# Attention and experts on one core: the weighted values of groups three and four joined, and the values' product moved behind the first two distances

## The chip, the core and the metric

The kernel runs on one core of one Trainium2 chip, in one launch. The metric is the time of that launch on the device in microseconds (us). Engines are named as the profile names them: PE is TensorE (PEld its weight loads), DVE is VectorE, ACT is ScalarE, POOL is GpSimd, SP is SyncE, which here only issues DMAs.

## The reference

One transformer layer over 32 batches of 256 tokens with 128 features. The attention has 16 heads of 8 features and replaces softmax by a rational function of the shifted logits; the expert part has four experts, of which each token uses two.

```python
x = x + attn(layernorm(x))            # qkv = x @ w_qkv.T, 16 heads of 8
    attn = einsum('bhsd,bhtd->bhst', q, k) * hd ** -0.5
    d = attn - max(attn)              # d <= 0
    s = 1 / (1 - d * (1 - 0.5 * d * (1 - d / 3)))
    out = (s / sum(s)) @ v            # then @ w_out.T + b_out
x = x + ffn(layernorm(x))
    gates = top 2 of softmax(x @ router_w + router_b), normalized
    h = silu(x @ w1[e]) * (x @ w3[e]) # 128 -> 512, for e in 0..3
    out = sum_e gates[e] * (h @ w2[e])
```

## The kernel before

Each engine has its own instruction stream, written out by hand; they meet only through semaphores (`wait_ge`, `then_inc`). Nothing reorders the work, so the order of the calls in the code is the order on the engine.

A stage number n stands for one step of a pipeline over batches. In `first_half` of step n, TensorE works on three batches: the distances of batch n (the maximum minus each score, from the scores recomputed with the row maximum as one more term), the end of the attention of batch n - 1, and the expert products of batch n - 2. In `second_half` it makes the scores of batch n + 1 for their maxima, the down products of batch n - 2, the router of batch n - 1, and the first weighted values of batch n. Steps -2 to 3 and 28 to 31 are written out, steps 4 to 27 run as a loop of 12 passes with two steps each. From step 2 on the order is the same ("settled", `settled(n)`).

The names that matter here:

- `distances(i, off, u)` (matmuls on L1380), u = 0..7: two products of 512 columns into `sc`. For u > 1 it waits for `poly_ok`, the polynomial of unit u - 2, which read the same buffer. ScalarE squares the distance (`square`, L657), VectorE makes the polynomial from square and distance (`polynomial`, L906).
- `weighted_values(i, off, g)` (L1312), g = 0..3: the weights of group g times the values, eight products in 32-column form (each recorded twice, so x16), into `pv`. It waits for `p_ok`, which ScalarE raises after the `Exp` of group g (`weights_of`, L771). ScalarE copies `pv` away after the fourth group (`values_T_copied`, L694).
- `values()` (L1405): the values of batch n + 1 into `misc`, x4 records. ScalarE copies them (`values_copied`, L688) between the second square and `silu(1)`.
- `up_a_unit`, `up_b_unit` (both L1294): six products of 256 columns each, the two factors of the hidden layer for unit u. `up_a` is read by `silu` (L666), `up_b` by `hidden` (L898). `up_a_unit(u)` waits for `silu(u - 1)`, `up_b_unit(u)` for a hidden product before it.

At the seam of two steps TensorE runs, before the change: `up_a_unit(0)`, queries and keys, `weighted_values(2)`, `up_b_unit(0)`, then in the next step `values()`, `distance(0)`, `distance(1)`, `weighted_values(3)`, `ups(1)` (both units 1), `distance(2)`, `up_a_unit(2)`, `distance(3)`, `up_b_unit(2)`, `up_a_unit(3)`, `distance(4)`. ScalarE's order in the same stretch is `silu(0)`, `square(0)`, `square(1)`, the copy of the values, `silu(1)`, the copy of `pv`, `square(2)`, `silu(2)`, `square(3)`. VectorE's is `hidden(0)`, `polynomial(0)`, `polynomial(1)`, `hidden(1)`, `polynomial(2)`, `hidden(2)`, `polynomial(3)`.

Of the kernel before, what the change touches and what calls it, by code (L numbers as in the profile page):

```python
# [5 lines left out]
def attention_then_experts_kernel(nc: bass.Bass, x: bass.AP, w_qkv: bass.AP, w_out: bass.AP, b_out: bass.AP,  # L6
# [26 lines left out]
    B, S, D = x.shape  # L33
# [25 lines left out]
    with ctx:  # L59
# [193 lines left out]
        def no(i, off):  # L253
            return 2 * i + off

        def has(i, off):
            return not isinstance(i, int) or 0 <= no(i, off) < B

        def after(eng, s, count):

            if not isinstance(count, int) or count > 0:
                eng.wait_ge(s, count)

        def settled(n):

            return not isinstance(n, int) or n >= 2
# [1010 lines left out]
        def _(pe):  # L1277
# [19 lines left out]
            def weighted_values(i, off, g):  # L1297

                n, par = no(i, off), off % 2
                pe.wait_ge(p_ok, G * n + g + 1)  # L1300
                if g == 0:
                    pe.wait_ge(v_ok, n + 1)
                    after(pe, o_ok, n)
                    if has(i, off - 2):
                        pe.wait_ge(hid_ok, UP * (n - 1))
                    if has(i, off + 1):
                        pe.wait_ge(s_used, U * (n + 1) + 6)
                first = 16 - 16 * (g % 2)
                for c in range(C):
                    for j in range(4):  # L1310
                        at = (2 * c + j % 2) * S
                        last = nc.tensor.matmul(pv[32 * j:32 * j + 32, g // 2, :],  # L1312
                                                v_pad[par][:, c, 4 * g + j, first:first + 32],
                                                poly[:, 2 * g + j // 2, at:at + S], start=(g % 2 == 0 and c == 0),
                                                stop=(g % 2 == 1 and c == C - 1))
                last.then_inc(pv_full, 1)
# [9 lines left out]
            def up_a_unit(i, off, u):  # L1326
                m = no(i, off)
                after(pe, silu_ok, UP * m + u)
                if u == 0:
                    pe.wait_ge(xn2_lo_ok, m + 1)  # L1330
                up(u, up_a, w1_hi, w1_lo, a_full)

            def up_b_unit(i, off, u):
                m = no(i, off)
                if u < 3:
                    after(pe, hid_ok, UP * m + u)
                elif u == 3:
                    pe.wait_ge(o_ok, min(m + 2, B) if isinstance(i, int) else m + 2)
                else:
                    pe.wait_ge(hid_ok, UP * m + u - 1)  # L1340
                if u == 0:
                    after(pe, acc_ok, m)
                    pe.wait_ge(lg_ok, m + 1)
                up(u, b_bank[u], w3_hi, w3_lo, b_full)
# [39 lines left out]
            def first_half(i, off):  # L1384
                n = no(i, off)

                def ups(u):
                    if has(i, off - 2):
                        up_a_unit(i, off - 2, u)
                        up_b_unit(i, off - 2, u)  # L1390

                def distance(u):
                    if has(i, off):
                        distances(i, off, u)

                def values():
                    if not has(i, off + 1):
                        return
                    m = n + 1
                    if isinstance(i, int) and m == 0:  # L1400
                        pe.wait_ge(qk_ok, 1)
                    else:
                        pe.wait_ge(qk_out, m)
                    for c in range(C):
                        last = nc.tensor.matmul(misc[:, c * D:(c + 1) * D], xn_T[:, c * 128:(c + 1) * 128],  # L1405
                                                proj_T[:, 2, :], start=True, stop=True)
                    last.then_inc(v_full, 1)
# [5 lines left out]
                def values_T():  # L1413
                    if not has(i, off - 1):
                        return
                    m = n - 1
                    pe.wait_ge(o_ok, m + 1)
                    if has(i, off + 1):
                        pe.wait_ge(v_ok, n + 2)
                    else:  # L1420
                        pe.wait_ge(xn2_out, m)
                        if has(i, off):
                            pe.wait_ge(m_ok, n + 1)
                    for c in range(C):
                        for a in range(G // 2):
                            at = (c * G // 2 + a) * 128
                            last = nc.tensor.transpose(misc[:, at:at + 128], o_T[:, a, c * 128:(c + 1) * 128], ident[:])  # L1427
                    last.then_inc(oq_full, 1)

                def attention_T():  # L1430
                    if not has(i, off - 1):
                        return
                    m = n - 1
                    pe.wait_ge(attn_ok, m + 1)
                    for c in range(C):
                        last = nc.tensor.transpose(misc[:, c * 128:(c + 1) * 128], attn[:, c, :], ident[:])
                    last.then_inc(attnT_full, 1)

                def output_projection():
                    if not has(i, off - 1):  # L1440
                        return
                    m = n - 1
                    pe.wait_ge(attnT_ok, m + 1)
                    for c in range(C):
                        last = nc.tensor.matmul(misc[:, c * D:(c + 1) * D], attn_T[:, c * 128:(c + 1) * 128],  # L1445
                                                proj_T[:, 3, :], start=True, stop=True)
                    last.then_inc(res_full, 1)

                if settled(n):
                    values()  # L1450
                    distance(0)
                    distance(1)
                    weighted_values(i, off - 1, 3)
                    ups(1)
                    distance(2)
                    up_a_unit(i, off - 2, 2)
                    distance(3)
                    up_b_unit(i, off - 2, 2)
                    up_a_unit(i, off - 2, 3)
                    distance(4)  # L1460
                    values_T()
                    up_a_unit(i, off - 2, 4)
                    distance(5)
                    up_b_unit(i, off - 2, 3)
                    up_b_unit(i, off - 2, 4)
                    up_a_unit(i, off - 2, 5)
                    distance(6)
                    attention_T()
                    up_a_unit(i, off - 2, 6)
                    distance(7)  # L1470
                    up_b_unit(i, off - 2, 5)
                    up_a_unit(i, off - 2, 7)
                    up_b_unit(i, off - 2, 6)
                    up_b_unit(i, off - 2, 7)
                    output_projection()
                    return
# [51 lines left out]
            def second_half(i, off):  # L1528
                n = no(i, off)
# [108 lines left out]
                if settled(n):  # L1638
                    score(0)
                    down(0, 0)  # L1640
                    down(0, 1)
                    score(1)
                    down(0, 2)
                    down(0, 3)
                    down(1, 0)
                    score(2)
                    down(1, 1)
                    down(1, 2)
                    router_operand()
                    score(3)  # L1650
                    down(1, 3)
                    if has(i, off + 2):
                        queries_operand()
                    weighted_values(i, off, 0)
                    weighted_values(i, off, 1)
                    if has(i, off + 1):
                        maxima_T()
                    router_logits()
                    up_a_unit(i, off - 1, 0)
                    if has(i, off + 2):  # L1660
                        queries_and_keys()
                    if isinstance(i, int) and n == B - 1:
                        up_b_unit(i, off - 1, 0)
                        late_up_a(LATE, 1)
                        late_up_b(LATE, 1)
                    weighted_values(i, off, 2)
                    if not (isinstance(i, int) and n == B - 1):
                        up_b_unit(i, off - 1, 0)
                    return

# [154 lines left out]
```

## Time and profile before

| what | value |
|---|---|
| median of 3 runs | 1122.63 us (1122.23 to 1123.55) |
| the profiled execution's own time | 1123.23 us |
| its span | 1121.5 us |
| granted TensorE clock, mean | 0.998 |
| PE busy | 1099.9 us (98%) |
| ACT busy | 995.3 us (89%) |
| DVE busy | 962.8 us (86%) |
| POOL busy | 744.1 us (66%) |
| one step in the middle of the kernel | 33.2 us |

The busy rows say how much of the span each engine had an instruction in flight. Matmuls overlap in the pipeline, so a PE that reads 98% busy can still be waiting a little between two of them; what tells is the distance from the start of one matmul to the start of the next. The last row is the distance between the same instruction in two neighbouring steps: the third group's weighted values start at 549.55 us in one step, and the row of the first two groups at 545.37 us has its like one step later at 578.53 us.

### The profile page before, as it was taken

How to read it: one execution, taken by the hardware profiler on the slowest of the kernel's cores; microseconds unless marked ns; L12 is line 12 of the kernel's file. 1: busy time of each engine (PE TensorE's matmuls, PEld its weight loads, DVE VectorE, ACT ScalarE, POOL GpSimd, SP SyncE). 2: the span in 40 equal slices, each digit the busy share in tenths (PEclk: the TensorE clock that was granted, in tenths of full speed). 3: DMA queues.
4: the chain of work that ended last, by engine and by line, in shares of the span. 5: the costliest groups of instructions: out<-in, count | busy, mean ns of one | idle time of the engine just before them, and what ended most of it. 6: DMA issues, size and time to landing. Idle time of an engine off the chain costs nothing.

```text
span 1121.5 us, 29146 instructions
## 1 busy us (share of the span) xinstructions
PE 1099.9 (98%) x9968; PEld 934.8 (83%) x9968; DVE 962.8 (86%) x1665; ACT 995.3 (89%) x1034; POOL 744.1 (66%) x936
## 2 busy tenths in 40 slices
PE   6989999999999999999999999999999999999998
PEld 5768888888888888888888888888888888888888
DVE  5789888899888899888899988889988889998844
ACT  1789999999999999999999999999999999999982
POOL 4547766777676687776677767668767667776530
PEclk9999999999999999999999999999999999999999
DMA  6343433333433223343223343322433322344000
GB/s 192 110 143 120 129 105 96 95 103 122 123 115 101 90 87 122 123 128 105 90 88 110 118 127 114 98 91 90 122 123 123 107 88 88 113 122 125 30 7 10
DMA packets 130383, 117.49 MB, mean 105 GB/s; under 512 B 15748, under 2 KB 124964, under 8 KB 130340
## 3 DMA queue, kind: packets, MB, share of 16 engines
q1 hardware_dynamic: 128004, 113.78, 32.9%
q10 hardware_dynamic: 2336, 3.15, 0.9%
q8 instruction: 26, 0.43, 0.2%
q14 instruction: 17, 0.14, 0.0%
HBM read 94.18 MB, written 21.09 MB: 103 GB/s over the span
## 4 chain that ended last, share of the span: by engine, by line
PE 93%; DVE 3%; ACT 1%; ACTq 1%; DMA 1%; issue 0%; POOL 0%; SPq 0%; POOLq 0%; DVEq 0%
PE banks L1294 33%; PE banks L1569 20%; PE sc L1380 11%; PE banks L1312 11%; PE sc L1552 4%; PE misc L1294 2%; PE banks L1603 2%; DVE mx L991 1%; PE misc L1427 1%; PE misc L1445 1%; PE misc L1405 1%; PE banks L1552 1%; PE sc L1294 1%; PE banks L1288 1%; DVE poly L906 1%; PE sc L1745 1%
## 5 line engine op out<-in xcount | busy, mean ns | idle before, releaser
L481 POOL TENSOR_TENSOR hid<-hid,gate_all 128x512 f32<-128x512 f32 x240 | 380.7, 1630 | 167.6 <-DMA gate_all<-gate_scratch 156.8
L906 DVE SCALAR_TENSOR_TENSOR poly<-w_sq,sc 128x1024 f32<-128x1024 f32 x252 | 303.5, 1215 | 46.3 <-ACT w_sq L657 46.1
L1294 PE MATMUL banks<-xn_hi,w_hi 128*128 128x256 f32 x976 | 289.5, 297 | 0.3
L1294 PE MATMUL banks<-xn_lo,w_hi 128*128 128x256 f32 x976 | 275.2, 282 | 0.0
L1294 PE MATMUL banks<-xn_hi,w_lo 128*128 128x256 f32 x976 | 274.1, 281 | 0.0
L657 ACT ACTIVATE w_sq<-sc 128x1024 f32<-128x1024 f32 x252 | 255.6, 1027 | 13.0 <-PE sc L1380 7.0
L1569 PE MATMUL banks<-w_sb,hid 128*128 128x128 f32 x1920 | 245.9, 281 | 0.4 <-POOL hid L481 0.4
L766 ACT ACTIVATE poly<-poly 128x2048 f32<-128x2048 f32 x128 | 240.2, 1899 | 0.3
L1569 PEld LDWEIGHTS banks<-w_sb,hid 128*128 128x128 f32 x1920 | 223.3, 191 | 16.5 <-POOL hid L481 0.6
L771 ACT ACTIVATE poly<-poly 128x2048 f32<-128x2048 f32 x128 | 236.8, 1896 | 0.0
L991 DVE TENSOR_REDUCE mx<-sc 128x4 f32<-128x1024 f32 x192 | 229.4, 1211 | 6.5 <-PE sc L1552 5.7
L1294 PEld LDWEIGHTS banks<-xn_hi,w_hi 128*128 128x128 f32 x976 | 183.3, 188 | 37.2 <-issue 24.3
L666 ACT ACTIVATE silu_a<-banks 128x512 f32<-128x512 f32 x240 | 144.1, 600 | 60.9 <-PE banks L1294 44.5
L1294 PEld LDWEIGHTS banks<-xn_lo,w_hi 128*128 128x128 f32 x976 | 183.8, 188 | 5.1
L1294 PEld LDWEIGHTS banks<-xn_hi,w_lo 128*128 128x128 f32 x976 | 184.2, 189 | 0.0
L898 DVE TENSOR_TENSOR hid<-silu_a,banks 128x512 f32<-128x512 f32 x240 | 161.0, 681 | 16.5 <-ACT silu_a L666 16.0
L1380 PE MATMUL sc<-q_pad,k_stack 128*128 128x512 f32 x504 | 161.2, 411 | 1.5 <-DMA q_pad<-m_split 0.8
L1312 PE MATMUL banks<-poly,v_pad 128*32 128x256 f32 x2048 | 130.6, 384 | 0.9 <-DVE mx L991 0.7
L1312 PEld LDWEIGHTS banks<-poly,v_pad 128*32 128x32 f32 x2048 | 56.7, 109 | 50.6 <-issue 17.9
L1380 PEld LDWEIGHTS sc<-q_pad,k_stack 128*128 128x128 f32 x504 | 78.8, 189 | 9.2 <-issue 1.9
L991 DVE TENSOR_REDUCE mx<-banks 128x4 f32<-128x1024 f32 x64 | 77.6, 1212 | 0.0
L1552 PE MATMUL sc<-k_tile,q_tile 32*128 32x256 f32 x768 | 64.6, 328 | 4.2 <-DVE mx L991 3.7
(186 smaller groups left out, 1338.2 us busy)
## 6 DMA issues: line engine op xcount, KB each, us to landing
qk_scratch<-qk_split SPq DMA_DIRECT2D x32, 512.0 KB, 3.1
q_pad<-qk_scratch SPq DMA_DIRECT2D x256, 64.0 KB
k_tile<-qk_scratch SPq DMA_DIRECT2D x124, 128.0 KB, 2.5
q_tile<-qk_scratch SPq DMA_DIRECT2D x124, 128.0 KB, 2.5
k_stack<-qk_scratch SPq DMA_DIRECT2D x124, 128.0 KB
gate_all<-gate_scratch SPq DMA_DIRECT2D x30, 512.0 KB, 4.4
x_in<-in_L_attn_x_dram SPq DMA_DIRECT2D x32, 128.0 KB, 2.1
x_res<-in_L_attn_x_dram SPq DMA_DIRECT2D x32, 128.0 KB, 2.2
```

The costliest lines, as they stand in the source:

```text
L481: nc.gpsimd.tensor_tensor(h, h, by_token.unsqueeze(1).to_broadcast([128, 2, C, 128]), ALU.mult).then_inc(gated, 1)
L657: nc.scalar.activation(w_sq[:, u % 2, :], distance_buf(n, u), ACT.Square).then_inc(sq_ok, 1)
L666: nc.scalar.activation(silu_a[:, u % 2, :], up_a[:], ACT.Silu).then_inc(silu_ok, 1)
L766: nc.scalar.activation(poly[:, C * g:C * (g + 1), :], poly[:, C * g:C * (g + 1), :], ACT.Ln, bias=2.0).then_inc(ln_ok, 1)
L771: nc.scalar.activation(poly[:, C * g:C * (g + 1), :], poly[:, C * g:C * (g + 1), :], ACT.Exp, scale=-1.0).then_inc(p_ok, 1)
L898: nc.vector.tensor_tensor(hid[:, 2 * u:2 * u + 2, :].rearrange("p a t -> p (a t)"), silu_a[:, u % 2, :], b_bank[u], ALU.mult).then_inc(hid ...
L906: nc.vector.scalar_tensor_tensor(poly[:, u, :], w_sq[:, u % 2, :], 3.0, distance_buf(n, u), ALU.add, ALU.mult).then_inc(poly_ok, 1)
L991: nc.vector.tensor_reduce(by_row[:, :, :, u], score_buf[u].rearrange("p (j c t) -> p j c t", j=2, c=C), AX.X, ALU.min, negate=True).then_i ...
L1294: last = nc.tensor.matmul(dst, lhs[a], rhs[b], start=(k == 0), stop=(k == len(terms) - 1))
L1312: last = nc.tensor.matmul(pv[32 * j:32 * j + 32, g // 2, :], v_pad[par][:, c, 4 * g + j, first:first + 32], poly[:, 2 * g + j // 2, at:at ...
L1380: last = nc.tensor.matmul(dst[:, 2 * c * S:2 * (c + 1) * S], k_stack[par][:, u, c * 128:(c + 1) * 128], q_pad[par][:, u, :, :].rearrange(" ...
L1569: last = nc.tensor.matmul(up_b[:, c * D:(c + 1) * D], hid[:, FB * e + f, c * 128:(c + 1) * 128], w2_sb[:, FB * e + f, :], start=(e == 0 an ...
```

## The change

In settled steps the third group's weighted values leave the second half, where they stood between queries and keys and `up_b_unit(0)`. They now open the next step's first half, directly followed by the fourth group's. Then come the first two distances, and behind those the values' product. In step 2 only the fourth group moves, since step 1 has already done the third group at the end of its own second half. In the last step (31) the third group stays in the second half. No product is added or dropped, and no wait is added: each call brings its own waits along.

```diff
                 if settled(n):
-                    values()
+                    if not (isinstance(i, int) and n == 2):
+                        weighted_values(i, off - 1, 2)
+                    weighted_values(i, off - 1, 3)
                     distance(0)
                     distance(1)
-                    weighted_values(i, off - 1, 3)
+                    values()
                     ups(1)
                     distance(2)
...
                         up_b_unit(i, off - 1, 0)
                         late_up_a(LATE, 1)
                         late_up_b(LATE, 1)
-                    weighted_values(i, off, 2)
-                    if not (isinstance(i, int) and n == B - 1):
+                        weighted_values(i, off, 2)
+                    else:
                         up_b_unit(i, off - 1, 0)
                     return
```

On TensorE, at the seam of two settled steps, this stands before (the first row is the last product of queries and keys; x8 of L1312 is one group, x4 of L1380 are distances 0 and 1):

```order
L1294 MATMUL misc<-xn_split,proj_lo 128x256
L1312 MATMUL banks<-poly,v_pad 32x256 x8
L1294 MATMUL banks<-xn_hi,w_hi 128x256
L1294 MATMUL banks<-xn_lo,w_hi 128x256
L1294 MATMUL banks<-xn_hi,w_lo 128x256
L1294 MATMUL banks<-xn_hi,w_hi 128x256
L1294 MATMUL banks<-xn_lo,w_hi 128x256
L1294 MATMUL banks<-xn_hi,w_lo 128x256
L1405 MATMUL misc<-proj_T,xn_T 128x128 x2
L1380 MATMUL sc<-q_pad,k_stack 128x512 x4
L1312 MATMUL banks<-poly,v_pad 32x256 x8
L1294 MATMUL banks<-xn_hi,w_hi 128x256
```

And this stands there now, again on TensorE and from the same product on:

```order
L1294 MATMUL misc<-xn_split,proj_lo 128x256
L1294 MATMUL banks<-xn_hi,w_hi 128x256
L1294 MATMUL banks<-xn_lo,w_hi 128x256
L1294 MATMUL banks<-xn_hi,w_lo 128x256
L1294 MATMUL banks<-xn_hi,w_hi 128x256
L1294 MATMUL banks<-xn_lo,w_hi 128x256
L1294 MATMUL banks<-xn_hi,w_lo 128x256
L1312 MATMUL banks<-poly,v_pad 32x256 x16
L1380 MATMUL sc<-q_pad,k_stack 128x512 x4
L1405 MATMUL misc<-proj_T,xn_T 128x128 x2
L1294 MATMUL banks<-xn_hi,w_hi 128x256
```

The two groups of eight have become one of sixteen that stands between the six products of `up_b_unit(0)` and the distances, and the values' product has moved from in front of the distances to behind them. This happens in steps 3 to 31, 29 times. The orders of the other engines are the same as before.

## Rows read from the trace of the kernel before

**Rows 1.** The page: the chain that ended last, by engine and by line.

```profile
PE 93%; DVE 3%; ACT 1%; ACTq 1%; DMA 1%; issue 0%; POOL 0%; SPq 0%; POOLq 0%; DVEq 0%
```

**Rows 2.** The waits: engine, line, what it waited for: us, times, longest us.

```profile
DVE poly L906 <- ACT w_sq L657: 46.1, 91, 3.4
```

**Rows 3.** The timeline of PE: start us, us, engine line op, tiles, shape, xcount.

```profile
545.37 1.93 PE L1312 MATMUL banks<-poly,v_pad 128*32 128x256 f32 x32
547.12 0.39 PE L1613 MATMUL misc<-ident,mx 128*32 128x128 f32 x4
...
549.34 0.28 PE L1294 MATMUL misc<-xn_split,proj_lo 128*128 128x256 f32 x1
549.55 1.07 PE L1312 MATMUL banks<-poly,v_pad 128*32 128x256 f32 x16
550.55 0.38 PE L1294 MATMUL banks<-xn_hi,w_hi 128*128 128x256 f32 x1
...
551.36 0.61 PE L1405 MATMUL misc<-proj_T,xn_T 128*128 128x128 f32 x4
551.72 0.71 PE L1380 MATMUL sc<-q_pad,k_stack 128*128 128x512 f32 x2
...
552.82 1.07 PE L1312 MATMUL banks<-poly,v_pad 128*32 128x256 f32 x16
553.82 0.39 PE L1294 MATMUL banks<-xn_hi,w_hi 128*128 128x256 f32 x1
...
555.36 0.62 PE L1380 MATMUL sc<-q_pad,k_stack 128*128 128x512 f32 x2
555.82 0.28 PE L1294 MATMUL banks<-xn_hi,w_hi 128*128 128x256 f32 x1
...
556.53 0.62 PE L1380 MATMUL sc<-q_pad,k_stack 128*128 128x512 f32 x2
556.99 0.28 PE L1294 MATMUL banks<-xn_hi,w_hi 128*128 128x256 f32 x1
...
558.44 0.73 PE L1380 MATMUL sc<-q_pad,k_stack 128*128 128x512 f32 x2
559.01 0.60 PE L1427 MATMUL misc<-ident,o_T 128*128 128x128 f32 x4
```

**Rows 4.** The timeline of PE in step 1, where a distance stands directly behind weighted values.

```profile
62.75 1.07 PE L1312 MATMUL banks<-poly,v_pad 128*32 128x256 f32 x16
63.75 0.73 PE L1380 MATMUL sc<-q_pad,k_stack 128*128 128x512 f32 x2
```

**Rows 5.** The timeline of ACT at the same seam; in brackets idle time and who ended it.

```profile
546.69 3.70 ACT L771 ACTIVATE poly<-poly 128x2048 f32<-128x2048 f32 x2
...
551.80 0.60 ACT L666 ACTIVATE silu_a<-banks 128x512 f32<-128x512 f32 x1
552.47 1.94 ACT L657 ACTIVATE w_sq<-sc 128x1024 f32<-128x1024 f32 x2
554.29 0.38 ACT L688 COPY v_pad<-misc 128x256 f32<-128x256 f32 x1
554.84 0.60 ACT L666 ACTIVATE silu_a<-banks 128x512 f32<-128x512 f32 x1 [0.17 <-PE banks L1294]
555.34 0.58 ACT L694 COPY o_T<-banks 128x512 f32<-128x512 f32 x1
556.02 1.03 ACT L657 ACTIVATE w_sq<-sc 128x1024 f32<-128x1024 f32 x1
...
563.08 0.60 ACT L666 ACTIVATE silu_a<-banks 128x512 f32<-128x512 f32 x1 [1.11 <-PE banks L1294]
```

**Rows 6.** The timeline of DVE at the same seam.

```profile
553.64 2.35 DVE L906 SCALAR_TENSOR_TENSOR poly<-w_sq,sc 128x1024 f32<-128x1024 f32 x2 [0.46 <-ACT w_sq L657]
555.91 0.68 DVE L898 TENSOR_TENSOR hid<-silu_a,banks 128x512 f32<-128x512 f32 x1
557.17 1.22 DVE L906 SCALAR_TENSOR_TENSOR poly<-w_sq,sc 128x1024 f32<-128x1024 f32 x1 [0.58 <-ACT w_sq L657]
```

## The prediction

> **What bounds the kernel now.** I read the chain of waits first. 93% of the span lies on PE [rows 1], so a microsecond of TensorE's order is a microsecond of the kernel unless something else holds TensorE back. Then I laid the timelines of PE, ACT and DVE side by side at one seam between two steps, since the 28 others look alike.
>
> On PE [rows 3] the reader is to see two things. First, what a visit to the 32-column form costs. From the last product of queries and keys (549.34) to the values (551.36) are 2.02 us. Seven steps of ordinary products lie in there; six of them take 0.71 (555.82 to 556.53), seven 0.83. So the third group adds 2.02 - 0.83 = 1.19 us to PE. Sixteen records take 1.00 from their start to the next matmul (549.55 to 550.55). Thirty-two take 1.75 (545.37 to 547.12), and there the next matmul is in the same 32-column form. That is eight rounds of four columns at 0.22 each. Four more rounds in one block therefore cost 4 x 0.216 = 0.86.
>
> Second, PE is not free. Distance 4 starts at 558.44. DVE's polynomial 2, for which it waits, starts at 557.17 and takes 1.22 [rows 6]: it ends at 558.39, 0.05 before. So in every step PE meets at distance 4 a chain distance - square - polynomial - distance that runs through three engines. The pair of products there takes 0.57 to the next matmul (558.44 to 559.01) where distance 2 takes 0.46 (555.36 to 555.82) [rows 3]. A distance whose wait ends just in time is thus 0.11 dearer. DVE's longest wait is for the squares [rows 2], which fits.
>
> **The change, part by part.**
>
> *Joining the groups.* Two visits of 1.19 become one of 1.19 + 0.86: PE saves 0.33 us a step. That holds in 29 steps, 9.6 us in all. The Trainium skill (TensorEngine Tiling, Key Properties) says that changing the tiling mode drains TensorE, while another tile in the same mode does not. The rows agree: 0.21 instead of 0.12 into the form, and 0.14 over four rounds out of it. By that rule alone the kernel would get 9.6 us faster; that is the first rival.
>
> *Is the wait for the weights covered?* The third group needs the third Exp, the fourth the last Exp. Both stand in the row at 546.69, which ends at 550.39 [rows 5]. The new block starts behind six products: 549.34 + 0.12 + 0.59 + 0.21 = 550.26, and its second half 0.88 later, at 551.14. The fourth group has 0.7 us of cover, and the third group's Exp is the earlier half of that row. Nothing is lost here.
>
> *Distance 0 comes later.* It now starts at 550.26 + 1.00 + 0.86 = 552.12 instead of 551.72. Its two products take 0.73 to the end behind weighted values [rows 4], against 0.71 behind the values [rows 3]. It ends at 552.85 instead of 552.43, 0.42 later. Before, `square(0)` started 0.04 after that end, at 552.47, and ACT had been idle since 552.40 [rows 5]: nothing there hides the delay. `square(0)` starts at 552.89. It takes 1.03, DVE starts 0.14 after it (553.50 to 553.64 before), and polynomial 0 takes 1.22 [rows 6]. It ends at 555.28 and releases distance 2 at 555.33.
>
> *The values.* Four records, 0.36 us, on either side of the distances: no price on PE. ACT copies them behind `square(1)`, now at 552.89 + 1.82 = 554.71. The product is done by 553.15 + 0.61 = 553.76. Covered by 0.9 us. If that cover were gone, `silu(1)` behind the copy would be late.
>
> *PE meets distance 2.* The four products of distances 0 and 1 took 1.10 (551.72 to 552.82), of which 0.09 was the way into the 32-column form; with the 0.02 above they take 1.03. So the values start at 553.15 and `up_a_unit(1)` at 553.51, 0.31 earlier than the 553.82 of before. Twelve products took 1.54 behind weighted values (553.82 to 555.36) and should take 1.52 here. PE arrives at 555.03 and waits 0.30 for 555.33. The saving is gone: before, distance 2 started at 555.36. And it now starts just in time, which the row of distance 4 prices at 0.11. The lower bound for that price is nothing, as at distance 2 before; I take 0.11, because the nearest row is the same instruction in the same state. So `up_a_unit(2)` comes at 555.33 + 0.57 = 555.90 instead of 555.82. From here on PE is 0.08 late.
>
> *Does it catch up?* `square(2)` needs the end of distance 2, 555.33 + 0.73 = 556.06, and starts at 556.10 (556.02 before). ACT gets there in time. It was idle 0.17 before `silu(1)` and 0.10 before `square(2)` [rows 5]. Copy and silu overlap what follows by some 0.1 (`silu(1)` at 554.84 takes 0.60, the next starts 0.50 later), which gives 554.98, 555.48 and 555.96. If no overlap were left behind the two copies it would be 556.17. Polynomial 2 starts at 557.25 and ends at 558.47, distance 4 starts at 558.52. PE itself comes there at 555.90 + 0.71 + 0.46 + 1.45 = 558.52. Hidden 1 ends at 557.01 and `up_b_unit(2)` comes at 557.07, just behind it. Both paths say 0.08 late, against 558.44. Distance 4 paid its 0.11 before already. Behind it, ACT idles 1.11 us for PE [rows 5], so the other engines follow PE, and the step ends 0.08 to 0.10 later. I take 0.09.
>
> *The sum.* 29 x 0.09 = 2.6 us slower. Step 2 has no join; the same late distance there is in the noise. The profiled execution took 1123.23, which gives 1125.8. The median of the runs lies 0.6 under it, so 1125.2 us.
>
> **The rivals.**
>
> *A. The join pays in full.* Nothing in front of distance 4 holds PE, and the tie there relaxes too: 1122.6 - 9.6 = 1113.0 us. For it speaks the chain of waits with 93% PE. Against it speak the squares: distance 0 moves 0.40 the wrong way and feeds the chain that PE already meets at distance 4. Partial gains (the polynomial starting sooner behind the square, say) belong here, between 1113 and 1120.
>
> *B. Even.* PE waits at distance 2, but no just-in-time price follows. Then PE is 0.03 early and the rest repeats: 29 x -0.03 = -0.9, 1121.7 us. For it speaks that the price was seen at one kind of place only; against it, that a distance is what will stand there.
>
> *C. ACT is dense.* The two copies overlap nothing, `square(2)` starts at 556.17, distance 4 at 558.59 and later, and the hidden product 1, 0.42 late and just in time for `up_b_unit(2)`, costs its own restart of up to 0.1: 0.2 a step, 1128.4 us. It decides from the point where ACT's two gaps (0.17 and 0.10) no longer take up the delay.
>
> **How the numbers follow.** The forecast has 0.47, A 0.12, B 0.24, C 0.17. The forecast's own range is 1123.6 to 1127.2 (0.03 to 0.16 a step). The full range goes from 1120.6, below B, to 1129.0, above C; it leaves out most of A and a tail of C. Changes within 0.2%, 2.2 us, can't be told from none: that is 1120.4 to 1124.9. Faster is A, 0.12. The same is B and a quarter of the forecast, 0.36. Slower is the rest, 0.52.
>
> **What would show it.** Right: per step the 32 records in one block of 1.86 us to the next matmul; `square(0)` 0.4 later against queries and keys; a PE pause of 0.3 in front of distance 2, whose pair then takes 0.73 and not 0.62; a step of 33.3 us. Wrong: distance 2 earlier than 5.7 us behind the end of queries and keys, a pair of 0.62 there, or PE waiting for an Exp in the joined block. If TensorE shows no pause at distance 2, the forecast is wrong as a whole; if the pause is there and the step is not longer, it is B.

## The result, and the profile after

The changed kernel takes 1125.42 us in the median of 15 runs (1123.91 to 1127.24), the kernel before 1123.07 (15 runs, 1122.23 to 1124.83). The ratio is 1.0022, with a 95% interval of 1.0014 to 1.0030: 2.4 us slower, where 1125.2 us was forecast. The profiled execution took 1126.04 us over a span of 1124.3, at a granted clock of 0.997 (before 0.998).

The step tells it without the ends of the kernel. The copy of queries and keys (L1005) runs once a step on DVE. Grouped by line, between 190 and 1010 us, the view gives its count, its min/median/max duration and its first and last start. Before:

```profile
L1005 DVE COPY qk<-misc x24: 690/692/692, 217.8 to 980.9; 128x512 f32<-128x512 f32 x24
```

After:

```profile
L1005 DVE COPY qk<-misc x24: 690/692/693, 219.0 to 983.8; 128x512 f32<-128x512 f32 x24
```

That is 763.1 / 23 = 33.18 us a step before and 764.8 / 23 = 33.25 after, 0.075 more. All steps below are worked out in this way. 29 x 0.075 is 2.2 us of the 2.8 by which the two spans differ. Between 190 and 1010 us the granted clock reads 1.00 in every profiled execution of this study, so the steps compare like with like. The first 100 us were granted 0.98 before and 0.97 after, which can be part of the other 0.6.

The chain that ended last has moved off PE in part. It was 93% PE [rows 1]:

```profile
PE 86%; ACT 5%; DVE 4%; issue 1%; ACTq 1%; DMA 1%; POOL 1%; SPq 0%; DVEq 0%; POOLq 0%
```

The waits (engine, line, what it waited for: us, times, longest) say the same of each step. DVE waits for the squares nearly as before [rows 2], 48.0 us in 91 times. What is new is that ACT's squares wait for distances and PE's weight loads for polynomials, each some 30 times, about once a step. After:

```profile
ACT w_sq L657 <- PE sc L1380: 22.6, 34, 3.8
PEld sc L1380 <- DVE poly L906: 11.2, 33, 0.7
```

Before:

```profile
ACT w_sq L657 <- PE sc L1380: 7.0, 6, 4.8
PEld sc L1380 <- DVE poly L906: 1.5, 3, 0.8
```

The timeline of PE at the same seam answers to [rows 3]. Its last product of queries and keys starts at 551.25, where it was 549.34 (unrounded, 1.915 apart), so 1.92 is to be taken off every time for a comparison.

```profile
551.25 0.28 PE L1294 MATMUL misc<-xn_split,proj_lo 128*128 128x256 f32 x1
...
552.18 1.93 PE L1312 MATMUL banks<-poly,v_pad 128*32 128x256 f32 x32
554.04 1.20 PE L1380 MATMUL sc<-q_pad,k_stack 128*128 128x512 f32 x4
555.08 0.61 PE L1405 MATMUL misc<-proj_T,xn_T 128*128 128x128 f32 x4
...
556.85 0.28 PE L1294 MATMUL banks<-xn_hi,w_lo 128*128 128x256 f32 x1
557.26 0.73 PE L1380 MATMUL sc<-q_pad,k_stack 128*128 128x512 f32 x2
557.83 0.28 PE L1294 MATMUL banks<-xn_hi,w_hi 128*128 128x256 f32 x1
...
558.53 0.63 PE L1380 MATMUL sc<-q_pad,k_stack 128*128 128x512 f32 x2
559.00 0.38 PE L1294 MATMUL banks<-xn_hi,w_hi 128*128 128x256 f32 x1
559.22 0.28 PE L1294 MATMUL banks<-xn_lo,w_hi 128*128 128x256 f32 x1
...
560.53 0.66 PE L1380 MATMUL sc<-q_pad,k_stack 128*128 128x512 f32 x2
561.02 0.60 PE L1427 MATMUL misc<-ident,o_T 128*128 128x128 f32 x4
```

The 32 records stand in one block, 1.86 to the next matmul. The last product in front of distance 2 starts at 556.85; the next would follow at 556.97 (0.12 later, as its like do), but distance 2 starts at 557.26: the pause is 0.29. Its pair then takes 0.57 to the next matmul, where it took 0.46.

ACT's timeline answers to [rows 5], in brackets the idle time and who ended it:

```profile
554.81 1.94 ACT L657 ACTIVATE w_sq<-sc 128x1024 f32<-128x1024 f32 x2 [0.51 <-PE sc L1380]
556.64 0.38 ACT L688 COPY v_pad<-misc 128x256 f32<-128x256 f32 x1
556.89 0.63 ACT L666 ACTIVATE silu_a<-banks 128x512 f32<-128x512 f32 x1
557.38 0.62 ACT L694 COPY o_T<-banks 128x512 f32<-128x512 f32 x1
558.03 1.03 ACT L657 ACTIVATE w_sq<-sc 128x1024 f32<-128x1024 f32 x1
```

And DVE's answers to [rows 6]:

```profile
555.99 2.35 DVE L906 SCALAR_TENSOR_TENSOR poly<-w_sq,sc 128x1024 f32<-128x1024 f32 x2 [0.90 <-ACT w_sq L657]
558.25 0.68 DVE L898 TENSOR_TENSOR hid<-silu_a,banks 128x512 f32<-128x512 f32 x1
559.18 1.22 DVE L906 SCALAR_TENSOR_TENSOR poly<-w_sq,sc 128x1024 f32<-128x1024 f32 x1 [0.24 <-ACT w_sq L657]
```

ACT idles 0.51 in front of `square(0)` and DVE 0.90 in front of polynomial 0 (0.46 before): the later distance 0 runs through both to distance 2.

### The profile page after: what moved, and what is told of

Read it like the earlier page. It is cut to its first block, busy times and chain, and to the rows that moved or that the text cites. A ratio compares the mean times of both kernels' runs of the same rounds, so it can differ in the third digit from the quotient of the medians.

```text
span 1124.3 us, 29134 instructions
## 1 busy us (share of the span) xinstructions
PE 1099.5 (98%) x9968; PEld 940.1 (84%) x9968; DVE 962.8 (86%) x1665; ACT 989.3 (88%) x1034; POOL 744.0 (66%) x936
## 4 chain that ended last, share of the span: by engine, by line
PE 86%; ACT 5%; DVE 4%; issue 1%; ACTq 1%; DMA 1%; POOL 1%; SPq 0%; DVEq 0%; POOLq 0%
PE banks L1294 29%; PE banks L1571 20%; PE sc L1380 11%; PE banks L1312 10%; PE sc L1554 4%; DVE poly L906 3%; ACT w_sq L657 2%; PE misc L1294 2%; PE banks L1605 2%; PE misc L1427 1%; PE misc L1445 1%; PE banks L1554 1%; PE sc L1294 1%; ACT poly L766 1%; PE banks L1288 1%
## 5 line engine op out<-in xcount | busy, mean ns | idle before, releaser
L1380 PE MATMUL sc<-q_pad,k_stack 128*128 128x512 f32 x504 | 162.7, 414 | 4.8 <-DVE poly L906 1.0
L1312 PE MATMUL banks<-poly,v_pad 128*32 128x256 f32 x2048 | 124.6, 382 | 1.0 <-DVE mx L991 0.7
L1380 PEld LDWEIGHTS sc<-q_pad,k_stack 128*128 128x128 f32 x504 | 78.4, 188 | 28.8 <-issue 13.7
L1312 PEld LDWEIGHTS banks<-poly,v_pad 128*32 128x32 f32 x2048 | 59.6, 109 | 45.3 <-issue 7.0
```

Of the source, the lines that this page charges most:

```text
L1312: last = nc.tensor.matmul(pv[32 * j:32 * j + 32, g // 2, :], v_pad[par][:, c, 4 * g + j, first:first + 32], poly[:, 2 * g + j // 2, at:at ...
L1380: last = nc.tensor.matmul(dst[:, 2 * c * S:2 * (c + 1) * S], k_stack[par][:, u, c * 128:(c + 1) * 128], q_pad[par][:, u, :, :].rearrange(" ...
```

## The experiments

Nine more kernels ran, timed beside the kernel before on the same chip; its median was 1123.81 us for the first four, 1122.90 for the next four and 1123.46 for the last. Steps are from the profiled executions. In e3, e4 and e5 a part of the squares is left out, so they don't compute the layer; the others do.

| kernel | median us | ratio to before (95%) | step us |
|---|---|---|---|
| before | | 1 | 33.18 |
| the change | 1125.42 | 1.0022 (1.0014 to 1.0030) | 33.25 |
| e1 values moved, no join | 1123.46 | 0.9999 (0.9990 to 1.0008) | 33.21 |
| e2 join, values stay in front | 1148.05 | 1.0212 (1.0198 to 1.0226) | 34.05 |
| e3 the change, squares of unit 0 halved | 1114.91 | 0.9916 (0.9902 to 0.9929) | 32.86 |
| e4 before, squares of unit 0 halved | 1122.99 | 0.9993 (0.9984 to 1.0002) | 33.19 |
| e5 before, squares of units 2 and 3 halved | 1119.14 | 0.9963 (0.9949 to 0.9976) | 33.03 |
| e6 join behind both distances | 1134.85 | 1.0106 (1.0091 to 1.0122) | 33.57 |
| e7 e6 with a spread tail | 1126.14 | 1.0027 (1.0017 to 1.0037) | 33.29 |
| e8 before with the spread tail | 1115.35 | 0.9933 (0.9919 to 0.9946) | 32.91 |
| e9 the change with the spread tail | 1116.70 | 0.9942 (0.9929 to 0.9956) | 33.00 |

### The two halves of the change

**e1: the values alone.**

```diff
-                    values()
                     distance(0)
                     distance(1)
+                    values()
                     weighted_values(i, off - 1, 3)
```

> Half of the change: in settled steps the order is distance 0, distance 1, values, weighted values of group 4; group 3 stays in the second half, so nothing is joined. Theory (the change loses its gain because distance 0 comes 0.4 us later and its square and polynomial hold up distance 2): here distance 0 comes 0.36 us earlier than before, TensorE has as many visits to the 32-column form as before, and the tie at distance 4 stays. No change: 1121.5 to 1124 us, the step 33.15 to 33.2 us. Rival (the values' product behind the distances is what costs, through its copy ahead of silu 1): the 0.09 us a step of the changed kernel show here too, 1125 to 1126 us.

Ratio 0.9999 (0.9990 to 1.0008), step 33.21, in the expected range. By itself the move of the values costs 0.03 a step, and nothing that the medians show.

**e2: the join alone**, with the values' product still first.

```diff
                 if settled(n):
                     values()
+                    if not (isinstance(i, int) and n == 2):
+                        weighted_values(i, off - 1, 2)
+                    weighted_values(i, off - 1, 3)
                     distance(0)
                     distance(1)
-                    weighted_values(i, off - 1, 3)
...
```

The second hunk of the change, which takes the third group out of the second half, comes with it.

> The other half: groups 3 and 4 joined, but the values' product stays in front: values, weighted values 3 and 4, distance 0, distance 1. Theory: distance 0 starts 0.36 us later still, 0.78 us behind before at its square. Polynomial 0 then releases distance 2 at 555.69 instead of 555.36 on the scale of the trace of before, plus the just-in-time price of 0.11, and hidden product 1 holds up the second b product with another restart: 0.44 to 0.8 us a step, 1135 to 1146 us. Rival (the joined block gains its 0.33 us and the move of the values loses it again): 1113 to 1116 us.

1148.05 us and 0.87 a step: the sign as expected, but above the range of 1135 to 1146. The theory had 0.36 for the values in front and no wait of theirs. PE at a seam:

```profile
562.36 0.71 PE L1405 MATMUL misc<-proj_T,xn_T 128*128 128x128 f32 x4
563.00 1.93 PE L1312 MATMUL banks<-poly,v_pad 128*32 128x256 f32 x32
564.87 1.19 PE L1380 MATMUL sc<-q_pad,k_stack 128*128 128x512 f32 x4
```

The copy of queries and keys starts there at 561.62 on DVE, takes 0.69, and the values start 0.05 behind its end: without group 3 in front of them they wait for it. The block starts 0.64 behind the values. Against the copy, distance 0 starts at 564.87 - 561.62 = 3.25; in the changed kernel it is 554.04 - 551.57 = 2.47. So the values in front cost 0.78 there: 0.36 for themselves, the rest for their wait and for the extra time that their first products take behind it (their restart). ACT's line shows where that goes:

```profile
565.64 1.94 ACT L657 ACTIVATE w_sq<-sc 128x1024 f32<-128x1024 f32 x2 [1.28 <-PE sc L1380]
```

1.28 idle in front of `square(0)`, where the change has 0.51; the difference is that 0.77 once more, and 34.05 - 33.25 = 0.80 is what the step grows by. From this point a delay of distance 0 is passed on in full. The second half of the change is thus what keeps the first from costing 24 us.

### The pause and its price

**e3: the change, with half the squares of unit 0**, so that the polynomial of distance 0 comes earlier while PE's order stays.

```diff
-                    nc.scalar.activation(w_sq[:, u % 2, :], distance_buf(n, u),
+                    width = 2 * S if settled(n) and u in (0,) else 4 * S
+                    nc.scalar.activation(w_sq[:, u % 2, 0:width], distance_buf(n, u)[:, 0:width],
...
```

> The changed kernel, but from step 2 on ScalarE squares only the first 512 of the 1024 columns of distance unit 0; the other half of those squares is left out. The square should take 0.60 instead of 1.03 us, so polynomial 0 releases distance 2 some 0.43 us sooner, 0.1 us before TensorE comes there. Theory: the pause of 0.4 us in front of distance 2 goes and the join pays its 0.33 us: 29 x 0.42 = 12 us under the changed kernel, 1112 to 1117 us. Rival (the price lies on TensorE itself, in the joined block or in the values behind the distances): 1124 to 1126 us.

1114.91 us, in the expected range, and a step of 32.86: 0.39 less than the change and 0.32 less than before. PE (its lines are one further down here):

```profile
545.34 1.93 PE L1313 MATMUL banks<-poly,v_pad 128*32 128x256 f32 x32
547.20 1.20 PE L1381 MATMUL sc<-q_pad,k_stack 128*128 128x512 f32 x4
548.24 0.61 PE L1406 MATMUL misc<-proj_T,xn_T 128*128 128x128 f32 x4
...
550.00 0.28 PE L1295 MATMUL banks<-xn_hi,w_lo 128*128 128x256 f32 x1
550.12 0.62 PE L1381 MATMUL sc<-q_pad,k_stack 128*128 128x512 f32 x2
550.58 0.28 PE L1295 MATMUL banks<-xn_hi,w_hi 128*128 128x256 f32 x1
```

Distance 2 follows without a pause (0.12 behind the product in front of it) and takes 0.46. Everything up to there is as in the changed kernel: 1.86 from the block to distance 0, 1.04 to the values. ACT's squares have shrunk:

```profile
547.97 1.52 ACT L658 ACTIVATE w_sq<-sc 128x512 f32<-128x512 f32 x2 [0.49 <-PE sc L1381]
```

and DVE waits 0.46 instead of 0.90 for them:

```profile
548.72 2.35 DVE L907 SCALAR_TENSOR_TENSOR poly<-w_sq,sc 128x1024 f32<-128x1024 f32 x2 [0.46 <-ACT w_sq L658]
```

Pause and price are 0.29 + 0.11 = 0.40 a step; 0.39 came back.

**e4: the same edit on the kernel before**, as a control.

> The control: the kernel before with the same half of the squares of unit 0 left out. Theory: nothing waits for polynomial 0 there (it ends at 554.86 and distance 2 starts at 555.36), so 1121.5 to 1123.5 us. Rival (any relief of ScalarE or VectorE shortens the step in either kernel): as much faster as in the changed kernel, 1111 to 1114 us.

1122.99 us, in the expected range: ratio 0.9993 (0.9984 to 1.0002), step 33.19. Halving that square gives nothing by itself, so what e3 gained is the wait of the changed kernel.

**e5: the kernel before, with half the squares of units 2 and 3.** Distances 4 and 5, which wait for those polynomials, are the two pairs that read 0.57 there.

```diff
+                    width = 2 * S if settled(n) and u in (2, 3) else 4 * S
...
```

The rest of the edit is as in e3.

> The kernel before, but from step 2 on ScalarE squares only the first 512 of the 1024 columns of units 2 and 3; the other half of those squares is left out. Polynomials 2 and 3 then end about 0.4 us sooner, and distances 4 and 5, which in the kernel before start 0.05 us after those polynomials, no longer start just in time. Theory (a distance that starts just behind its wait is 0.11 us dearer, even where the pause in front of it is nearly nothing): two prices go, 0.15 to 0.22 us a step, 1117 to 1119.5 us, and the pairs of distances 4 and 5 take 0.46 us to the next matmul and not 0.57. Rival (the 0.57 belongs to what stands behind the pair, the transposes, or is drawn from the record only): at most the few hundredths of the pause, 1121.5 to 1123.5 us.

1119.14 us, ratio 0.9963 (0.9949 to 0.9976), step 33.03. In the expected range.

```profile
556.38 0.62 PE L1381 MATMUL sc<-q_pad,k_stack 128*128 128x512 f32 x2
556.84 0.60 PE L1428 MATMUL misc<-ident,o_T 128*128 128x128 f32 x4
...
558.05 0.62 PE L1381 MATMUL sc<-q_pad,k_stack 128*128 128x512 f32 x2
558.52 0.28 PE L1295 MATMUL banks<-xn_hi,w_hi 128*128 128x256 f32 x1
```

Distance 4 takes 0.46 instead of 0.57 [rows 3], and distance 5 takes 0.47 instead of 0.57. So the price of the just-in-time start is the wait's, not the place's. The two pairs are 0.21 shorter together, the step 0.15: the rest was given back elsewhere, and where stays open.

### Other places for the join

**e6: the values first, then both distances, then the join.** That leaves distance 0 without a block in front of it.

```diff
                 if settled(n):
                     values()
                     distance(0)
                     distance(1)
+                    if not (isinstance(i, int) and n == 2):
+                        weighted_values(i, off - 1, 2)
                     weighted_values(i, off - 1, 3)
...
```

The diff is against the kernel before; the second hunk of the change comes with it.

> The join with the distances in front of it: values, distance 0, distance 1, weighted values of groups 3 and 4. Distance 0 is ready 1.2 us sooner than before, so no square is late. Theory: the 0.33 us of the join stay, less a new wait: with the third group gone from in front of it, the values' product comes 0.87 us sooner, at 550.17 on the scale of before, and waits for the copy of queries and keys, which DVE ends at 550.34: 0.2 to 0.25 us. Net 0.07 to 0.12 us a step, 1119.5 to 1121.5 us. Rival (the join itself is worth nothing, and only the order of the distances counted): 1122.5 to 1126 us, with the new wait paid and nothing for it.

1134.85 us, 0.39 a step slower than before: outside what either theory gave. There are two new waits (PE's and its weight loads' view). The theory had the first; neither had the second:

```profile
PEld misc L1405 <- DVE qk L1005: 8.3, 29, 0.4
PE sc L1380 <- DMA q_pad<-m_split: 4.9, 14, 1.6
PEld sc L1380 <- DMA q_pad<-m_split: 2.5, 12, 0.2
```

The first is the values' wait for the copy of queries and keys: 0.28 of the weight load in each of 29 steps. On PE it is 0.22, the 0.2 to 0.25 of the theory: the copy starts at 554.60 and the values at 555.34, 0.74 behind, where in the changed kernel the block behind the same product starts 0.61 behind the copy's start (552.18 - 551.57), 0.09 of it being the way into the 32-column form. The second is a DMA. SP moves the row maxima into the queries' tile, and with less work between, distance 0 reaches it:

```profile
553.12 0.61 SPq L437 DMA_DIRECT2D q_pad<-m_split  x1
...
555.34 0.71 PE L1405 MATMUL misc<-proj_T,xn_T 128*128 128x128 f32 x4
556.06 0.76 PEld L1380 LDWEIGHTS sc<-q_pad,k_stack 128*128 128x128 f32 x4 [0.20 <-DMA q_pad<-m_split]
556.06 1.20 PE L1380 MATMUL sc<-q_pad,k_stack 128*128 128x512 f32 x4
```

2.94 us from issue to use. Before the change it was 3.54 for the same DMA: 551.72 [rows 3] minus

```profile
548.18 0.61 SPq L437 DMA_DIRECT2D q_pad<-m_split  x1
```

so group 3's block stood as cover for both the copy and this transfer. The distances follow the values by 0.72 instead of 0.36. This is the cheaper of two kinds of step that alternate. One step later the DMA is issued at 586.69, and it takes 3.06 to its use:

```profile
588.81 0.71 PE L1405 MATMUL misc<-proj_T,xn_T 128*128 128x128 f32 x4
589.75 1.17 PE L1380 MATMUL sc<-q_pad,k_stack 128*128 128x512 f32 x4 [0.23 <-DMA q_pad<-m_split]
```

0.94 there. Over the 24 steps between 190 and 1010 us the joined block starts 1.94 behind the values in the mean, where before a block started 1.46 behind them (552.82 - 551.36): 0.48 more. The saving of 0.33 is overrun by 0.22 and 0.48 at these two places, which makes 0.37 of the 0.39. Not all of the 0.48 is the transfer's. In e2, where no transfer is in the way, the values behind their wait take 0.64 - 0.36 - 0.09 = 0.19 more than usual; my estimate is that some 0.3 is left for the transfer. That the transfer ends the wait is the profile's attribution; a kernel with this DMA issued earlier was not tried.

**e7: e6 with a spread tail.** The tail of the first half is the edit of e8 below.

> The order of the run before this one, and behind it the rest of the first half spread so that more of TensorE's own work stands between a distance or a product and what it waits for: b unit 3 in front of distance 5, the transpose of the attention in front of a unit 5, b unit 4 in front of a unit 6, the output projection between a unit 7 and b unit 6. Theory: what holds TensorE in a step besides its own work is a set of short waits for ScalarE and VectorE; in the kernel before it waits in front of a unit 6 for silu 5 (0.2 us) and just in time in front of distances 4 and 5 (0.11 us each). With these gone: 0.3 to 0.45 us a step under before, 1109 to 1115 us. Rival (TensorE is full, and the order behind distance 2 is worth nothing): the time of the join behind the distances, 1119.5 to 1121.5 us.

1126.14 us, ratio 1.0027 (1.0017 to 1.0037). That is above the ranges of both theories, since both counted e6's join as a gain. The waits of e6 are there again: 8.3 us in 29 times for the copy of queries and keys, and for the transfer 4.8 us in 15 times on PE and 2.5 in 12 on its weight loads. Against e6 the tail gives 0.28 a step.

**e8: the kernel before with the spread tail.** `up_b_unit(3)` covers distance 5, and the two short jobs at the end move to places where a wait stood.

```diff
                     up_a_unit(i, off - 2, 4)
-                    distance(5)
                     up_b_unit(i, off - 2, 3)
-                    up_b_unit(i, off - 2, 4)
+                    distance(5)
+                    attention_T()
                     up_a_unit(i, off - 2, 5)
                     distance(6)
-                    attention_T()
+                    up_b_unit(i, off - 2, 4)
                     up_a_unit(i, off - 2, 6)
                     distance(7)
                     up_b_unit(i, off - 2, 5)
                     up_a_unit(i, off - 2, 7)
+                    output_projection()
                     up_b_unit(i, off - 2, 6)
                     up_b_unit(i, off - 2, 7)
-                    output_projection()
```

`ups(1)` is written out as its two calls as well, with the same products.

> The kernel before with the spread order of the first half alone; groups 3 and 4 stand where they stood before, two visits to the 32-column form. Theory: the short waits go and the join's 0.33 us, less the 0.23 of the wait for queries and keys, is missing: 0.1 us a step above the joined and spread kernel, 1112 to 1117 us. Rival (once the short waits are gone the join pays in full): 0.33 us a step, about 9.6 us, above the joined and spread kernel.

1115.35 us, ratio 0.9933 (0.9919 to 0.9946), step 32.91: in the expected range, and by median and step the fastest kernel of this study that computes all of the layer. It was also expected to be 0.1 a step slower than e7; it is 0.38 faster, because e7 pays for the transfer of e6. PE, first the piece before, at distances 5 and 6:

```profile
560.17 0.73 PE L1380 MATMUL sc<-q_pad,k_stack 128*128 128x512 f32 x2
560.74 0.28 PE L1294 MATMUL banks<-xn_hi,w_hi 128*128 128x256 f32 x1
...
563.34 0.38 PE L1436 MATMUL misc<-ident,attn 128*128 128x128 f32 x2
563.73 0.39 PE L1294 MATMUL banks<-xn_hi,w_hi 128*128 128x256 f32 x1
```

and in e8:

```profile
556.43 0.63 PE L1380 MATMUL sc<-q_pad,k_stack 128*128 128x512 f32 x2
556.90 0.39 PE L1436 MATMUL misc<-ident,attn 128*128 128x128 f32 x2
557.04 0.37 PE L1294 MATMUL banks<-xn_hi,w_hi 128*128 128x256 f32 x1
```

Before, `up_a_unit(6)` stood 0.39 behind the transposes, because `silu(5)` ended at 563.68 [rows 5]; in e8 the product behind the transposes follows by 0.14. With the 0.10 of distance 5 (0.57 to 0.47) that is 0.35; the step got 0.27 of it.

**e9: the change with the same tail.**

> The changed kernel (groups 3 and 4 joined in front of distances 0 and 1, values behind) with the spread order behind distance 2, which alone made the kernel before 7.6 us faster. Theory: the late distance 0 holds up distance 2 and hidden product 1 here as it did without the spread, since both stand in front of the part that is spread. So the change costs 0.07 to 0.1 us a step on this base too: 2 to 4 us above the spread kernel, 1117 to 1120 us. Rival (in the changed kernel only the crowded part behind distance 2 turned the join's 0.33 us into nothing): with that part spread the join pays, 1106 to 1113 us.

1116.70 us, just under the expected 1117 to 1120; ratio 0.9942 (0.9929 to 0.9956), step 33.00. In the medians it is 1.35 us above e8, and the two intervals overlap, so the times alone don't tell them apart. The steps do: with the spread tail the change costs 0.08 a step (791.9 / 24 against 789.9 / 24), as it does without (0.075). Distance 2 comes 0.41 behind the product in front of it and takes 0.57, as in the change. The loss is made in front of distance 2 and is not taken up behind it.

## Why the prediction was right

Times of the changed kernel are shifted by 1.92 here, so that they stand beside those of the prediction.

1. **The join: right.** 0.33 a step was forecast. With the pause gone, e3 is 0.32 a step faster than before, 1123.81 - 1114.91 = 8.9 us in the medians, where 9.6 was the sum. The Trainium skill (TensorEngine Tiling (Array Packing), Key Properties) says that a change of the tiling mode drains TensorE; e3, with one such visit less in each step, agrees. With the wait in place the 9.6 us don't show: rival A is wrong for this kernel.
2. **The weights are covered: right.** The block starts at 550.26, as forecast.
3. **Distance 0 later by 0.40: right.** 552.12 forecast and measured, `square(0)` 552.89 both.
4. **The pause: right.** 555.33 forecast for distance 2, 555.34 measured; a pause of 0.30 forecast, 0.29 measured.
5. **The just-in-time price: right.** 0.57 to the next matmul, forecast 0.57. e5 confirmed that it goes with the wait. Rival B needed it to be absent.
6. **Behind distance 2: two terms off, against each other.** Hidden 1 ends at 558.25 + 0.68 = 558.93 and `up_b_unit(2)` starts at 559.00, with a restart: 0.22 to its second product, where 0.12 is ordinary. The forecast had hidden 1 just ahead of it and gave that 0.1 to rival C alone. So distance 4 starts at 558.61, 0.17 late instead of 0.08. But polynomial 2 ends at 559.18 + 1.22 = 560.40, 0.13 before distance 4 at 560.53 (unshifted), so the wait has slack again: its pair takes 0.49, not 0.57 (560.53 to 561.02), and behind it PE is 559.10 against 559.01, 0.09 late. The forecast said that distance 4 keeps its price. The two errors, 0.10 and 0.08, nearly cancel. They are linked, since PE's later arrival is what gives polynomial 2 its slack. But the forecast had neither, so at this place the number is right by luck.
7. **The rest of the step: right.** ACT idles 1.11 in front of `silu(5)` as before [rows 5], now at 565.09, shifted 563.17 against 563.08: 0.09 late. Over many steps the mean is 0.075, where 0.09 was taken: the term is a little too large, 2.2 us instead of 2.6 over 29 steps. The forecast of 1125.2 starts from a median of 1122.6 for the kernel before; over 15 runs that median is 1123.07, so a part of the agreement with 1125.42 is chance as well.
8. **C: half right.** Its restart is there. ACT is dense too, but `square(2)` at 556.11 is where the forecast had it (556.10) and not where C had it (556.17), and 0.2 a step did not come of it.

The values in front or behind: e1 bears out that they cost next to nothing by themselves; what the prediction did not see is how much they would cost in front of the joined block (e2), since it did not ask.

## What to carry to other kernels

Before counting what a join of two blocks saves, write down what comes later because of it: here 0.33 us a step was saved behind a start that moved 0.40 the wrong way, at the head of a chain of three engines that already met TensorE at its next link. Lay the timelines of all three side by side from one anchor and carry each delay until it is taken up. A pair of products that reads 0.57 where its like reads 0.46 marks a wait with no slack; such marks show where reordering pays (e8). And a block that looks in the way may be the cover of a copy and a transfer (e6).

## What the runs showed of the hardware that was not expected

- A product whose wait ends just in time costs about 0.1 us even where PE shows no pause. Taking it away at two places gave 0.15 us a step (e5).
- The same four values' records take 0.36 us to the next matmul behind finished operands and 0.64 behind the copy they wait for (e2), of which 0.09 is the way into the 32-column form.
- The small transfer `q_pad<-m_split` takes 2.94 us from its issue to its use in one step and 3.06 in the next where it is waited for (e6). Before the change it had 3.54 (551.72 - 548.18): some 0.5 us to spare.
